# Two-layer attention and expert kernel: the order of value products, scores and value projections in the attention rounds

## The reference

```
x = x + xattn(layernorm(x), ctx, w_q, w_k, w_v, w_o, b_o)   # 16 heads of 64
x = x + ffn(layernorm(x), ...)                              # routed + shared experts
...
q = x @ w_q;  k = ctx @ w_k;  v = ctx @ w_v                 # per head: 512x64, 1024x64, 1024x64
attn = softmax(q @ k.T * SCALE);  out = attn @ v;  return out.reshape(...) @ w_o + b_o
```

## Time and profile before

| | |
|---|---|
| median of 3 runs | 2855.45 us (2854.86 to 2857.53) |
| profiled execution | 2854.93 us, span 2853.1 us |
| TensorE matmul busy | 2645.7 us, 93% |
| VectorE busy | 2016.6 us, 71% |
| GpSimd busy | 1335.1 us, 47% |
| ScalarE busy | 1291.2 us, 45% |

### The profile page before, as it was taken

How to read it: one execution, slowest core, us unless ns; L and a number is a source line. 1 busy time by engine, 2 the same in 40 slices (tenths; PEclk the granted TensorE clock), 3 DMA queues, 4 the chain that set the end, 5 groups by cost and what they waited for, 6 DMA issues and landing times. The chain is left out here.

```text
span 2853.1 us, 41026 instructions
## 1 busy us (share of the span) xinstructions
PE 2645.7 (93%) x13254; PEld 1812.8 (64%) x13254; DVE 2016.6 (71%) x2808; ACT 1291.2 (45%) x1891; POOL 1335.1 (47%) x1054
## 2 busy tenths in 40 slices
PE   3999999999999879999999689999999999996895
PEld 2556565655656458888888555656565656554785
DVE  5677676767676578777777657677776777764795
ACT  3545454554545333333333344545454545443384
POOL 4565656565656501111111145666656565652245
PEclk9999999999999989999999789999999999997997
DMA  3111111111101020000000010111111111102312
GB/s 109 36 34 29 33 27 35 31 32 29 40 22 35 12 71 22 22 28 22 22 22 22 10 39 23 41 29 33 29 33 29 37 26 37 28 23 116 120 50 86
DMA packets 48851, 108.86 MB, mean 38 GB/s; under 512 B 7200, under 2 KB 22432, under 8 KB 47776
## 3 DMA queue, kind: packets, MB, share of 16 engines
q1 hardware_dynamic: 43952, 101.01, 12.3%
q0 software_dynamic: 1536, 4.20, 0.5%
q10 hardware_dynamic: 3312, 3.02, 0.3%
HBM read 47.64 MB, written 10.22 MB: 20 GB/s over the span
## 5 line engine op out<-in xcount | busy, mean ns | idle before, releaser
L372 POOL TENSOR_TENSOR L1a_psums<-L1a_psums,L1a_probs 128x512 f32<-128x512 f32 x384 | 480.8, 1288 | 50.1 <-ACT L1a_probs L407 50.1
L372 POOL TENSOR_TENSOR L0a_psums<-L0a_psums,L0a_probs 128x512 f32<-128x512 f32 x384 | 480.7, 1288 | 49.8 <-ACT L0a_probs L407 49.8
L472 DVE TENSOR_REDUCE L1a_row_max<-psum 128x1 f32<-128x1024 f32 x256 | 301.6, 1220 | 145.0 <-PE psum L584 144.8
L472 DVE TENSOR_REDUCE L0a_row_max<-psum 128x1 f32<-128x1024 f32 x256 | 301.6, 1220 | 144.7 <-PE psum L584 144.5
L803 POOL TENSOR_TENSOR L0e_w_lo<-L0e_raw,L0e_w_hi 128x768 fp32r<-128x768 f32 x34 | 63.7, 1873 | 496.7 <-ACT L0e_w_hi L817 496.7
L407 ACT ACTIVATE L1a_probs<-psum 128x1024 f32<-128x1024 f32 x256 | 253.5, 1025 | 76.6 <-PE psum L612 75.1
L407 ACT ACTIVATE L0a_probs<-psum 128x1024 f32<-128x1024 f32 x256 | 253.5, 1025 | 75.4 <-PE psum L612 73.9
L625 PE MATMUL psum<-L0a_probs,L0a_v 128*64 128x512 f32 x1024 | 247.3, 605 | 0.0
L625 PE MATMUL psum<-L1a_probs,L1a_v 128*64 128x512 f32 x1024 | 247.3, 605 | 0.0
L857 DVE SCALAR_TENSOR_TENSOR xres<-psum,L0e_weights_of,xres 128x256 f32<-128x256 f32 x544 | 225.6, 477 | 22.6 <-PE psum L1030 21.8
L372 POOL TENSOR_TENSOR L1a_psums<-L1a_probs 128x512 f32<-128x512 f32 x64 | 81.3, 1290 | 321.4 <-ACT L1a_probs L407 321.4
(11 more groups left out here) (348 smaller groups left out, 6223.8 us busy)
## 6 DMA issues: line engine op xcount, KB each, us to landing
L0a_k_hs<-L0a_k_st SPq DMA_DIRECT2D x64, 256.0 KB, 3.6
L1a_k_hs<-L1a_k_st SPq DMA_DIRECT2D x64, 256.0 KB, 3.5
L0e_raw<-in_experts SPq DMA_DIRECT2D x34, 384.0 KB, 2.9
L1weights<-in_sorted SPq DMA_DIRECT2D x2, 6144.0 KB, 17.9
L0a_q_hh<-L0a_q_hh SPq DMA_DIRECT2D x64, 128.0 KB, 2.3
L1a_q_hh<-L1a_q_hh SPq DMA_DIRECT2D x64, 128.0 KB, 2.3
L0a_raw<-in_attention SPq DMA_DIRECT2D x8, 384.0 KB, 3.1
L1a_raw<-in_attention SPq DMA_DIRECT2D x8, 384.0 KB, 2.9
```

Of the source, the lines that this page charges most:

```text
L372: nc.gpsimd.tensor_tensor(psums[:, h, :], a, probs[:, h, kv, :], ALU.add).then_inc(sem["acc"], 1)
L472: nc.vector.reduce_max(row_max[:, qt, 32 * h:32 * h + 1], slot(h), axis=AX.X).then_inc(sem["max"], 1)
```

## The change

In a segment with `ahead`, one value product now stands ahead of the first round, and a round goes scores, two value products, value projection, where it went two value products, scores, value projection. The last round has one value product. In a segment without `ahead` the value products keep their order. In segments with `ahead` the waits of value products 2, 4 and 6 for their exponentials go away; these products now stand behind `score(0)`, which waits for all eight. No instruction is added or taken away otherwise.

```diff
-                        def pv(hp, b, kv, first=False):
+                        def pv(hp, b, kv, first=False, ahead=True):
                             par = b % 2
                             if kv == 0:
                                 if not first:
                                     pe.wait_ge(sem["norm"], count(hp, 1, b, 0))
                                 pe.wait_ge(sem["v"], count(hp, NV, b, NV))
-                            if kv % 2 == 0:
+                            if kv == 0 or not ahead and kv % 2 == 0:
                                 pe.wait_ge(sem["exp"], count(hp, 8, b, kv + 2))
...
                             qk(hp, b, 6)
                             qk(hp, b, 7)
+                            pv(hp, b, 0, first, ahead)
                             for qt in range(QT):
-                                pv(hp, b, 2 * qt, first)
-                                pv(hp, b, 2 * qt + 1, first)
                                 if ahead:
                                     score(hp, b + 1, qt)
+                                for kv in range(2 * qt + 1, min(2 * qt + 3, KVT)):
+                                    pv(hp, b, kv, first, ahead)
+                                if ahead:
                                     project_values(VALUES[qt], hp, b + 1, not first)
```

## The result

The changed kernel takes 2876.69 us (median of 4 runs, 2876.11 to 2878.9) against 2855.15 us for the kernel before (4 runs, 2853.58 to 2857.53): a ratio of 1.0073, 95% interval 1.0061 to 1.0084. It is slower by 21.5 us. The prediction was 2869.9 us in a range of 2858 to 2888. The sign and the range held; 14.4 us more were forecast and 21.5 came.

What follows compares the result with a forecast made beforehand. TensorE's instruction list and its waits were taken to bound the attention. +0.26 us in 60 segments (+15.6) less 1.2 in the last segments gave +14.4, 2869.9 us, range 2858 to 2888.

Steps and rivals of the forecast that it cites:

- What bounds the kernel: In the attention, time is the length of TensorE's instruction list plus the few places where it stands still.
- The product moved away from the front: At a segment's first scores: score(0) starts 0.67 us earlier, with a new 0.19 us wait for the last exponential.
- The rounds and VectorE: Scores still follow scores after 3.37 us; VectorE's reductions come 0.08 late but hold nothing, by 0.04 us.
- The rival in which the lone products and the wait at the front cost nearly nothing: Rounds reach 3.33 us, key projection 0.18 earlier than forecast; about the same time, 2859.1 us; chance 0.12.
- K: Start of the next segment's key projection on TensorE, 446.00 before the change, forecast at 446.33.
- The product moved to the end: Behind a segment's last scores, one value product of 1.01 us makes the next key projection start 0.33 us later.
- The wait at the transposes: TensorE's 0.47 us wait at L596 goes, but qk(0) waits 0.40 us for ScalarE's rows; only 0.07 is gained.
- the faster rival: Transposes' wait is a true gain if the max_rows rows come some 0.4 us sooner: −0.14 a segment, 2845.9 us; chance 0.08.
- The sum: +0.26 us in each of 60 segments, +15.6, less 1.2 in the layers' last segments: +14.4 us, 2869.9 us.
- The rest: Exponentials, sums, copies and output additions move with qk(0) or the key projection; waits removed from products 2, 4, 6 cost nothing.
- VectorE as the bound of every round: Rival: 0.2 us more in the copy's chain makes two scores a segment late, +19 us, 2889 us; chance 0.15.

Runs made afterwards that it cites:

- values_front: Changed kernel with the first value projection between the lone value product and score(0), later projections each one round earlier; ratio 1.0034 to the kernel before.
- pair_front: Changed kernel with two value products instead of one ahead of the first scores, none in the last round; 2868.14 us, ratio 1.0019 to the kernel before.
- rows_first_after: Changed kernel with ScalarE copying the two rows of the maxima ahead of its two key copies; 2848.27 us, ratio 0.9952 to the kernel before.
- split_early: Changed kernel with batch 2's weight split on ScalarE after exponential 5 instead of 7; 2874.32 us, ratio 1.0044 to the kernel before.

## Why the prediction was right, and where it was short

*What bounds the kernel.* Right. TensorE's list and its waits set the time, and a segment could be added up from distances between starts: 29.05 us were forecast for a regular one and 29.04 measured. Two readings of its parts were off all the same, as follows.

*The product moved away from the front.* The mechanism was right, the release was mis-sized: `score(0)` starts 1.28 us behind its product, where 1.20 were forecast. The exponentials end at 435.62 + 1.95 = 437.57 and the scores start 0.15 us later, not 0.06. So the new wait costs 0.27 us. values_front shows it as a cost of its own.

*The rounds and VectorE.* Right: 3.38, 3.37 and 3.38 us. The new joints cost what the old ones did, and the 0.04 us of margin held. pair_front shows this without the lone products. The rival in which the lone products and the wait at the front cost nearly nothing did not come: a lone product costs its 1.01 us, the rounds do not get down to 3.33, and K is later than forecast, not earlier.

*The product moved to the end.* It costs 1.00 us (448.51 to 449.51). K lies 450.26 − 436.44 = 13.82 us behind the first product, before 446.00 − 432.60 = 13.40: 0.42 later, where I had 0.33. The difference is the release above.

*The wait at the transposes.* The mechanism was right, and the point on which the sign hung. It was removed and came back at `qk(0)`. There the release of the rows was shorter than I took it: first row done at 452.89 + 0.59 = 453.48, `qk(0)` at 453.53, 0.05 us and not 0.14. `qk(0)` is at K + 3.27 instead of K + 3.36. The two errors in the releases have opposite signs and cancel: +0.26 a segment was forecast, +0.26 came by these distances (0.42 − 0.16), 0.25 by the segment's length. That they cancel is luck.

One size in this step was misread. The prediction took TensorE to be ready for the transposes at K + 1.37, by taking the profile's idle time of 0.47 us, which counts from the modelled end of a matmul, off the start. From start to start they begin at K + 1.21 once nothing holds them (450.26 to 451.47), and `total` begins 0.53 and not 0.58 us behind. So TensorE is ready for `qk(0)` at K + 2.74 (rows_first_after) and not at K + 2.96: the old wait was worth 0.63 us and the new one 0.53, where 0.47 and 0.40 were given. The forecast was not touched, since ScalarE's rows set `qk(0)` either way, but the faster rival was priced too low.

*The sum.* The step that failed is "The rest", which costed all work not named at nothing, and with it the sum's +0.26 us for all 60 segments alike. VectorE's weight split in the segments of batch 2 was not looked at. It stood ahead of the first reductions with 0.04 us between them and costs 0.25 to 0.31 us in each of 14 segments, about 4 us. split_early brings these segments down to the others' 29.02 to 29.07 us; over the stretch it takes off 3.2 us, as the other segments get up to 0.04 longer. With the rows first the same edit takes off 4.0. In the last segment of a layer the gain was 0.52 us, not 0.59. The two before it grew by 0.39 to 0.42 us from `qk(0)` to `qk(0)` and not by 0.25 (from 28.71 to 28.73 before, to 29.11 to 29.14 now), 0.6 us more in both layers together; this was not looked into.

The stretch from the second segment's `qk(0)` to the last one's lasts 872.48 us in layer 0 (104.14 to 976.62) against 863.58 before (103.90 to 967.48), and 872.56 against 863.55 in layer 1: together 17.9 of the 21.2 us by which the span grew. For this stretch the prediction had 13.9, and the weight split adds 4. That the two make exactly 17.9 is in part chance: the 0.6 just named and a regular segment at +0.25 cancel. The other 3.3 us lie outside: 2.3 between the layers (from 976.62 to 1708.25, 731.63 us, before 729.31), 0.7 behind layer 1 and 0.2 ahead of layer 0. Part of these stretches runs at the lower clock (the granted clock from 1600 to 1700 us is 0.73 before and 0.71 after, from 50 to 100 us 0.90 and 0.80), so they may belong to when the clock rose and not to the change. The last column of the table speaks for that: without any change to TensorE's order it moves by 9 us. So the 3.3 us are not shown to be the change's, and where exactly they come from stays open.

*The rivals.* The faster one (the transposes' wait as a true gain) did not come and is shown to be real under its own condition: with the rows started 0.79 us sooner behind K (K + 1.84, 446.06 to 447.90, where they stood at K + 2.63), the change does gain, some 0.25 us a segment where the prediction had priced it at 0.14. VectorE as the bound of every round did not come, but it did at one `score(1)` in four, by another piece of work in its queue.

## What to carry to other kernels

When a wait is removed, follow the next instruction that waits for the same chain and for its neighbours: here key copies stood ahead of two short rows on ScalarE, and `qk(0)` started only 0.16 us behind what they allowed (K + 3.43 against K + 3.27). Two late inputs hide each other, and only taking away both shows a gain; a change that "does nothing" or costs a little can be half of one that pays. And a segment that is read from one timeline is not every segment: before multiplying by 60, look for the work that only some of them have and ask by how much it fits.

## What the hardware showed unexpectedly

The time from the end of ScalarE's instruction to the start of the TensorE instruction that waited for it differs from place to place by 0.1 us: 0.05 us behind the rows, 0.14 behind the same instruction in the first segment, 0.06 between exponential and scores in the last segment, and 0.15 between exponential and `score(0)` in the changed kernel. One such value, taken from another place, is good to about 0.1 us and no better; over 60 segments that is 6 us.

A lone value product costs 1.01 us and a pair 1.87, so two blocks of one product cost about 0.15 us more than one block of two. values_front shows the other side: behind a lone product the keys' second record starts after 0.33 us instead of 0.29. The Trainium skill ("TensorEngine Tiling (Array Packing)", Key Properties) says that a change of tiling mode drains the engine; these numbers agree with it, though no run here shows that draining is the cause.
